# First self attention of a two-layer decoder: where in a group of four heads two pieces of projection work stand

## The chip, the cores and the metric

The kernel runs on one core of a Trainium2 chip. The metric is the device time of one execution in microseconds (us); where a kernel is timed, it is run several times and the median counts. The profile is of one execution, and its times are counted from the start of its span.

## The reference, cut to what matters

Two decoder layers with a layer norm behind each block. The change is in the first block, a self attention with 16 heads of 64 over 4 sequences of 1024 tokens of width 256:

```python
xq = jnp.einsum('bsh,oh->bso', x, wq)
xk = jnp.einsum('bsh,oh->bso', x, wk)
xv = jnp.einsum('bsh,oh->bso', x, wv)
# each reshaped to (bsz, N_HEADS, seqlen, HEAD_DIM)
scores = jax.nn.softmax(jnp.einsum('bhid,bhjd->bhij', xq, xk) * SCALE, axis=-1)
out = jnp.einsum('bhij,bhjd->bhid', scores, xv).reshape(bsz, seqlen, N_HEADS * HEAD_DIM)
x = _layernorm(x + jnp.einsum('bso,ho->bsh', out, wo))
```

The reshape doesn't transpose, so one "head" is 64 consecutive tokens with all their 1024 projected values: 1024 rows of 64. There are 64 such heads, each an attention of 1024 by 1024.

## The kernel before, in words

`layer0_self_attention` walks 16 groups of 256 tokens, and in each group 4 heads (`group`, j = 0 to 3, here called first to fourth). While a group's heads are computed, the projections of the next group (in the fourth head: of the one after it) are made in pieces between their matmuls.

**A head.** For each of 8 blocks of keys (kc): scores in two halves (`scores`, L627, "A" and "B" operands, hi and lo parts of fp32r), two matmuls of 512 columns each; between them `step`, which calls `largest` for the **next** head: a matmul (L579) into one of the two banks of `psX`, whose row maximum VectorE takes (L584). ScalarE exponentiates the scores (L639), GpSimd adds the exponentials up (`add_up`, L655, the first add behind the second exponential), and TensorE multiplies them with the values (`values`, L667) in two batches in the middle and one at the end. Then `take_out` copies the result, and `max_rows` transposes the next head's maxima (L594), VectorE takes their minimum (L599, L600) and `masked` (L609) writes them in two halves into `qB`, which the second half of the next head's scores reads. `masked` has two inputs in SBUF, `nT` and `rowmask`.

**Loads.** `build` (L538) issues from SP, right behind a head's last scores, six DMAs of 256 KB with the operands of the head after the next, into the buffers that the head has just left. The first four (`qA`, `kA`) are needed by the first `largest` of the next head (semaphore `a0` or `a1`). `build_v` (L562) loads the values of the next head in the middle of a head.

**Pieces.** `SLOTS` gives places in a group to tasks: 16 pieces Q and K (`misc`, L417: six matmuls of 256 columns, a copy `ph` on ScalarE, L458, the subtraction `pl` on VectorE, L462, and two stores of 128 KB from SP, L491), four pieces V (L425: six matmuls of 512 columns, a copy on ScalarE, L471), one T (transposes of x) and two O (output projection, L436). Places "k6", "k1" and so on stand behind that block's scores; "1", "2", "2b" in the middle; "3" to "3d" at the head's end, behind `max_rows`. A piece writes the bank `psM`, or `psX` 1 at "3b" and `psX` 0 at "3c". VectorE runs in program order; at the ends of the second and fourth head that order is: the subtraction of "3", the first mask, those of "3b" and "3c", the second mask, that of "3d".

**Waits for a bank.** VectorE's tasks on the pieces count up the semaphore `md`, ScalarE's alone (V, T) `ma`. `misc` lets TensorE wait for all of them but the last `back` ones: `under` counts how many pieces came since the one that used the same bank. `back` in `step` does the same for `largest`, whose banks are `psX` 0 and 1.

**Other work on VectorE.** In the second and fourth head `moments` (L498, L500) stands behind the second block's scores: layer norm statistics of an output tile. In the second head V stands there too ("k1").

Of the kernel before, what the change touches and what calls it, by code (L numbers as in the profile page):

```python
# [300 lines left out]
def layer0_self_attention(nc, x, wqT, wkT, wvT, woT, y):  # L301
# [13 lines left out]
    with ExitStack() as ctx:  # L315
# [44 lines left out]
        psX = m.ps("psX", [P, 2, 512])  # L360
# [8 lines left out]
        def task_list():  # L369

            slots = dict(zip(PLACES, QK, strict=True))
            slots[0, "3d"] = slots[2, "3b"] = ("O",)
            slots[2, "3"] = ("T",)
            for n, place in enumerate(((0, "k6"), (1, "k1"), (2, "k6"), (2, "k7"))):
                slots[place] = ("V", n // 2, n % 2)
            return slots

        AHEAD = 5
        QK = [("Q", c) for c in range(KC)] + [("K", c) for c in range(KC)]
        PLACES = [(3, "1"), (3, "3"), (3, "3b"), (3, "3c"), (3, "3d"), (0, "1"), (0, "2"), (0, "2b"), (0, "3"), (0, "3b"),  # L380
                  (1, "1"), (1, "3"), (1, "3b"), (1, "3c"), (1, "3d"), (2, "1")]
        SLOTS = task_list()

        def load_x(w, g):
# [182 lines left out]
        def largest(w, i, b, back=None):  # L567


            u, half = i // 2, i % 2  # L570
            if w.on("tensor"):
                if i == 0:
                    w.wait(f"fa{b}", 8 * 16)
                    w.wait(f"a{b}", w.at(f"a{b}"))
                    w.wait("mn", w.at("mn"))
                if back is not None:
                    w.wait("md", w.at("md", back))
                w.wait("mxr", w.at("mxr", 1))
                w.eng.matmul(psX[:, half, :], qA[:, b, u * P:(u + 1) * P], kA[:, b, half * 512:(half + 1) * 512],  # L579
                             start=True, stop=True).then_inc(sems["mx"], 1)  # L580
            w.inc("mx")
            if w.on("vector"):
                w.wait("mx", w.at("mx"))
                w.eng.tensor_reduce(nmax[:, half, u:u + 1], psX[:, half, :], AX.X, ALU.max, negate=True)\  # L584
                    .then_inc(sems["mxr"], 1)
            w.inc("mxr")
# [27 lines left out]
        def scores(w, kc, b, a):  # L614

            half = kc % 2
            if w.on("tensor"):
                if a == 0:
                    if kc == 0:
                        w.wait(f"fb{b}", 4 * 16)  # L620
                        w.wait(f"b{b}", w.at(f"b{b}"))
                    w.wait("e", w.at("e", 1))
                kt, qt = (kB, qB) if a else (kA, qA)
                for q in range(2):
                    if a and kc == 0:
                        w.wait("mb", w.at("mb", 1 - q))
                    last = w.eng.matmul(psS[:, half, q, :], kt[:, b, kc * P:(kc + 1) * P], qt[:, b, q * 512:(q + 1) * 512],  # L627
                                        start=a == 0, stop=a == 1)
                if a:
                    last.then_inc(sems["s"], 1)  # L630
            if a == 0:
                return
            w.inc("s")
            n = w.count.get("e", 0) % RING
            if w.on("scalar"):
                w.wait("s", w.at("s"))
                w.wait("pv", w.at("pv", {0: 3, 1: 2}.get(kc, 1 - kc % 2)))
                w.wait("ad", w.at("ad", 3 if kc in (0, 5, 6, 7) else 2))
                w.eng.activation(pr[:, n, :], psS[:, half, :, :].rearrange("p a b -> p (a b)"), ACT.Exp, scale=SCALE)\  # L639
                    .then_inc(sems["e"], 1)  # L640
            w.inc("e")
# [59 lines left out]
        def group(w, G, first=False, left=2):  # L701
            last = left == 0

            for j in range(GH):
                more = not (last and j == GH - 1)
                b, nb = j % 2, (j + 1) % 2
                old = not (first and j == 0)
                def step(i):
                    if not more:
                        return  # L710
                    before = (j - 1) % GH
                    back = None
                    if (i == 0 and (before, "3c") in SLOTS) or (i == 1 and (before, "3c") not in SLOTS):
                        back = int((before, "3d") in SLOTS and not (first and j == 1))
                    if i == 13 and (j, "2b") in SLOTS:
                        back = 0
                    largest(w, i, nb, back)

                def piece(where, bank=None, under=(0, 0)):


                    task = SLOTS.get((j, where))
                    ahead = 2 if task == ("T",) or j == 3 else 1
                    if task is None or (not old if task[0] == "O" else ahead > left):
                        return under
                    if task[0] == "O":
                        misc(w, task, G - (j == 0), 1 if j == 0 else 0, bank=bank, back=under)
                    else:
                        misc(w, task, G + ahead, (G + ahead) % 2, bank=bank, back=under)
                    return under[0] + int(task[0] in "QKO"), under[1] + {"T": 2, "V": 1}.get(task[0], 0)  # L730

                for p in range(KC // 2):
                    for kc in (2 * p, 2 * p + 1):
                        scores(w, kc, b, 0)
                        step(2 * kc)
                        scores(w, kc, b, 1)
                        add_up(w, kc, j % 2)
                        outs = j % 2 == 1 and not (first and j == 1)
                        if outs and kc == 2:
                            root(w, 1 if j == 1 else 0)  # L740
                        if outs and kc == 5:
                            norm_out(w, G - (j == 1), 1 if j == 1 else 0)
                        if kc == KC - 1 and not (last and j >= 2):
                            build(w, G + (j + 2) // GH, (j + 2) % GH, b)
                        step(2 * kc + 1)
                        if outs and kc == 1:
                            moments(w, 1 if j == 1 else 0)
                        piece(f"k{kc}")
                        if old and kc == 4:
                            turn_back(w)  # L750
                        if old and kc == 5:
                            divide(w, (j - 1) % GH)
                    if p == 1:
                        piece("1")
                    if p in (1, 2):
                        values(w, 2 * p - 2, b)
                        values(w, 2 * p - 1, b)
                        if p == 1 and old:
                            misc(w, ("S",), G, (j + 1) % 2)
                        if p == 1 and more:  # L760
                            build_v(w, (j + 1) % GH, nb)
                    if p == 2:
                        under = piece("2")
                        if w.on("tensor") and (j, "2b") in SLOTS:
                            w.wait("mxr", w.at("mxr"))
                        piece("2b", bank=psX[:, 1, :], under=under)
                for kc in range(KC - 4, KC):
                    values(w, kc, b)
                take_out(w)
                if more:  # L770
                    max_rows(w, nb)
                rest_first = left > 0 and SLOTS.get((j, "3"), ("T",))[0] in "QK"
                if more and not rest_first:
                    masked(w, nb, 0)
                    masked(w, nb, 1)
                first_d, first_a = under = piece("3")
                if more and rest_first:
                    masked(w, nb, 0)
                under = piece("3b", bank=psX[:, 1, :], under=under)
                if w.on("tensor") and (j, "3c") in SLOTS:  # L780
                    w.wait("mn", w.at("mn"))
                under = piece("3c", bank=psX[:, 0, :], under=under)
                if more and rest_first:
                    masked(w, nb, 1)
                piece("3d", under=(under[0] - first_d, under[1] - first_a))
                if j == 1 and not last:
                    load_x(w, G + 2)

# [2060 lines left out]
```

## Time and profile before

| | |
|---|---|
| median of 3 runs | 3000.15 us (2994.0 to 3001.02) |
| profiled execution | 2996.25 us, its span 2994.5 us |
| first self attention | from the start to about 1730 us |
| TensorE busy, share of the span | 88% |
| VectorE, ScalarE, GpSimd busy | 57%, 39%, 53% |
| granted clock, mean | 0.942 of full speed |

Rows of a timeline give the start in us, the duration in us, the engine, the line of the kernel, the operation, and what it writes and reads; xN joins N instructions of a kind that follow each other. Matmuls overlap in the array, so their durations are longer than the distance from one start to the next. In brackets stands the idle time of the engine before the row, and what ended it. PE is TensorE, DVE VectorE, ACT ScalarE, POOL GpSimd, SP the queue that issues DMAs; `a_` is the prefix of this stage's tiles.

### The profile page before, as it was taken

How to read it: one execution, taken by the hardware profiler on the slowest of the kernel's cores; microseconds unless marked ns; L12 is line 12 of the kernel's file. 1: busy time of each engine (PE TensorE's matmuls, PEld its weight loads, DVE VectorE, ACT ScalarE, POOL GpSimd, SP SyncE). 2: the span in 40 equal slices, each digit the busy share in tenths (PEclk: the TensorE clock that was granted, in tenths of full speed). 3: DMA queues.
4: the chain of work that ended last, by engine and by line, in shares of the span. 5: the costliest groups of instructions: out<-in, count | busy, mean ns of one | idle time of the engine just before them, and what ended most of it. 6: DMA issues, size and time to landing. Idle time of an engine off the chain costs nothing. (4 is left out here: it accounts for less than half of the span.)

```text
span 2994.5 us, 43256 instructions
## 1 busy us (share of the span) xinstructions
PE 2639.8 (88%) x11953; PEld 1603.3 (54%) x11953; DVE 1699.4 (57%) x3404; ACT 1175.7 (39%) x1644; POOL 1574.1 (53%) x1309
## 2 busy tenths in 40 slices
PE   7999999999999999999999968882796588788696
PEld 5666666666666666666666533432474244343254
DVE  5665665656666665665666634663234555468743
ACT  3443444444444444444444324541222334344234
POOL 3666766767766677676777731224333313222343
PEclk8999999999999999999999979996898599899798
DMA  6554455554556445455554320003894100000233
GB/s 174 115 130 111 105 121 114 120 116 110 113 114 135 108 111 120 106 121 114 122 115 106 68 82 9 2 2 116 334 339 144 45 0 1 30 2 9 49 124 91
DMA packets 407008, 303.17 MB, mean 101 GB/s; under 512 B 293559, under 2 KB 338911, under 8 KB 401791
## 3 DMA queue, kind: packets, MB, share of 16 engines
q1 hardware_dynamic: 390734, 231.17, 32.9%
q0 software_dynamic: 12224, 64.71, 6.1%
q10 hardware_dynamic: 3952, 6.08, 0.6%
q8 instruction: 50, 0.82, 0.1%
q14 instruction: 48, 0.39, 0.1%
HBM read 187.04 MB, written 94.39 MB: 94 GB/s over the span
## 5 line engine op out<-in xcount | busy, mean ns | idle before, releaser
L655 POOL TENSOR_TENSOR a_total<-a_total,a_pr 128x1024 f32<-128x1024 f32 x384 | 914.0, 2380 | 55.9 <-ACT a_pr L639 35.1
L639 ACT ACTIVATE a_pr<-a_psS 128x1024 f32<-128x1024 f32 x512 | 525.3, 1027 | 670.3 <-PE a_psS L627 666.5
L584 DVE TENSOR_REDUCE a_nmax<-a_psX 128x1 f32<-128x512 f32 x1024 | 695.4, 688 | 157.4 <-PE a_psX L579 155.8
L667 PE MATMUL a_psO<-a_pr,a_vd 128*64 128x512 f32 x2048 | 481.8, 602 | 0.0
L579 PE MATMUL a_psX<-a_kA,a_qA 128*128 128x512 f32 x1024 | 413.1, 405 | 25.6 <-issue 12.6
L655 POOL TENSOR_TENSOR a_total<-a_pr 128x1024 f32<-128x1024 f32 x64 | 153.5, 2399 | 482.0 <-ACT a_pr L639 482.0
L627 PE MATMUL a_psS<-a_qA,a_kA 128*128 128x512 f32 x1024 | 338.9, 412 | 2.7 <-DVE a_nT L600 1.4
L627 PE MATMUL a_psS<-a_qB,a_kB 128*128 128x512 f32 x1024 | 321.2, 395 | 0.0
L667 PEld LDWEIGHTS a_psO<-a_pr,a_vd 128*64 128x64 f32 x2048 | 129.9, 136 | 236.5 <-issue 179.3
L579 PEld LDWEIGHTS a_psX<-a_kA,a_qA 128*128 128x128 f32 x1024 | 194.0, 190 | 105.8 <-issue 35.9
L627 PEld LDWEIGHTS a_psS<-a_qA,a_kA 128*128 128x128 f32 x1024 | 180.9, 189 | 123.1 <-issue 90.1
L627 PEld LDWEIGHTS a_psS<-a_qB,a_kB 128*128 128x128 f32 x1024 | 193.2, 189 | 39.4 <-DVE a_qB L609 1.2
L1076 POOL CAST c_qR<-c_qF 128x512 fp32r<-128x512 f32 x64 | 39.4, 615 | 207.5 <-ACT c_qF L1071 207.5
L1092 DVE TENSOR_REDUCE c_nmx<-c_psM 128x4 f32<-128x308 f32 x256 | 110.1, 467 | 63.3 <-PE c_psM L1087 61.8
L599 DVE COPY a_nT<-a_psX 8x128 f32<-8x128 f32 x64 | 17.8, 279 | 222.3 <-PE a_psX L594 222.3
L1066 PE MATMUL c_psM<-c_xT,c_wq 128*128 128x512 f32 x256 | 120.3, 607 | 5.4 <-ACT c_xT L1053 5.4
L475 DVE STREAM_TRANSPOSE a_turned<-a_psM 128x512 f32<-128x512 f32 x64 | 45.9, 717 | 135.8 <-PE a_psM L430 135.8
L1087 PE MATMUL c_psM<-c_kblk,c_qR 128*128 128x308 f32 x256 | 92.7, 401 | 27.9 <-DVE c_nmx L1092 14.3
L677 ACT ACTIVATE a_oU<-a_psO 128x512 f32<-128x512 f32 x64 | 38.3, 599 | 184.1 <-PE a_psO L667 180.1
L462 DVE TENSOR_TENSOR a_pl<-a_psM,a_ph 128x256 fp32r<-128x256 f32 x150 | 63.1, 421 | 81.2 <-ACT a_ph L458 81.2
L1087 PEld LDWEIGHTS c_psM<-c_kblk,c_qR 128*128 128x128 f32 x256 | 46.1, 191 | 112.9 <-issue 91.3
L1215 POOL TENSOR_TENSOR c_rstd<-c_mv,c_eps 128x2 f32<-128x2 f32 x32 | 6.3, 196 | 186.6 <-DVE c_mv L1206 186.5
(390 smaller groups left out, 4344.7 us busy)
## 6 DMA issues: line engine op xcount, KB each, us to landing
a_qA<-a_qhi SPq DMA_DIRECT2D x124, 256.0 KB
a_vd<-a_vg SPq DMA_DIRECT2D x128, 128.0 KB
a_kA<-a_khi SPq DMA_DIRECT2D x62, 256.0 KB
a_kA<-a_klo SPq DMA_DIRECT2D x62, 256.0 KB
a_kB<-a_khi SPq DMA_DIRECT2D x62, 256.0 KB
a_qB<-a_qlo SPq DMA_DIRECT2D x62, 256.0 KB
a_qhi<-a_ph SPq DMA_DIRECT2D x120, 128.0 KB, 3.1
a_qlo<-a_pl SPq DMA_DIRECT2D x120, 128.0 KB, 2.9
```

The costliest lines, as they stand in the source:

```text
L462: w.eng.tensor_tensor(pl[:, n, :], ps[:, 0:GT], ph[:, n, :].bitcast(F32), ALU.subtract)\
L475: w.eng.transpose(turned[:, :], ps[:, :]).then_inc(sems["md"], 1)
L579: w.eng.matmul(psX[:, half, :], qA[:, b, u * P:(u + 1) * P], kA[:, b, half * 512:(half + 1) * 512], start=True, stop=True).then_inc(sems[" ...
L584: w.eng.tensor_reduce(nmax[:, half, u:u + 1], psX[:, half, :], AX.X, ALU.max, negate=True)\
L627: last = w.eng.matmul(psS[:, half, q, :], kt[:, b, kc * P:(kc + 1) * P], qt[:, b, q * 512:(q + 1) * 512], start=a == 0, stop=a == 1)
L639: w.eng.activation(pr[:, n, :], psS[:, half, :, :].rearrange("p a b -> p (a b)"), ACT.Exp, scale=SCALE)\
L655: w.eng.tensor_tensor(total[:, buf, :], first, pr[:, n, :], ALU.add).then_inc(sems["ad"], 1)
L667: last = w.eng.matmul(psO[q * HD:(q + 1) * HD, :], vd[:, b, kc, :], pr[:, n, q * 512:(q + 1) * 512], start=kc == 0, stop=kc == KC - 1)
L1066: last = w.eng.matmul(psM[:, k, :], wq[:, cc, c * P:(c + 1) * P], xT[:, cc, :], start=cc == 0, stop=cc == 1)
L1076: w.eng.tensor_copy(qR[:, n % 2, c, :], qF[:, n % 3, c, :]).then_inc(sems["qr"], 1)
L1087: w.eng.matmul(psM[:, k, 0:K4], qR[:, n % 2, c, tt * P:(tt + 1) * P], kblk[:, c, b, :, :].rearrange("p i k -> p (i k)"), start=True, stop= ...
L1092: w.eng.tensor_reduce(nmx[:, tt, 4 * c:4 * c + 4], psM[:, k, 0:K4].rearrange("p (i k) -> p i k", k=TK), AX.X, ALU.max, negate=True).then_i ...
```

## The change

Two things move. In the fourth head (j = 3) the piece Q at "1", in the middle, goes, and the five Q pieces stand at "3", "3b", "3c", "3d" and a new place "3e". In the second head (j = 1) the piece V at "k1" goes to "3d", and the K piece that was there to "3e". "3e" writes `psX` 1, the bank of "3b", and its `under` lets the two pieces since "3b" be open in the fourth head, one of each kind in the second: the subtraction of "3b" must be done. The first `largest` of the next head (`psX` 0) now lets the pieces behind "3c" be open, and the second (`psX` 1) waits for all of them.

```diff
-            for n, place in enumerate(((0, "k6"), (1, "k1"), (2, "k6"), (2, "k7"))):
+            for n, place in enumerate(((0, "k6"), (1, "3d"), (2, "k6"), (2, "k7"))):
...
-        PLACES = [(3, "1"), (3, "3"), (3, "3b"), (3, "3c"), (3, "3d"), (0, "1"), (0, "2"), (0, "2b"), (0, "3"), (0, "3b"),
-                  (1, "1"), (1, "3"), (1, "3b"), (1, "3c"), (1, "3d"), (2, "1")]
+        PLACES = [(3, "3"), (3, "3b"), (3, "3c"), (3, "3d"), (3, "3e"), (0, "1"), (0, "2"), (0, "2b"), (0, "3"), (0, "3b"),
+                  (1, "1"), (1, "3"), (1, "3b"), (1, "3c"), (1, "3e"), (2, "1")]
...
-                        back = int((before, "3d") in SLOTS and not (first and j == 1))
+                        later = [SLOTS[before, where][0] for where in ("3d", "3e") if (before, where) in SLOTS]
+                        back = sum(t in "QKO" for t in later) if not (first and j == 1) else 0
+                    elif i == 1 and (before, "3e") in SLOTS:
+                        back = 0
...
-                first_d, first_a = under = piece("3")
+                past_3 = piece("3")
...
-                under = piece("3b", bank=psX[:, 1, :], under=under)
+                past_3b = piece("3b", bank=psX[:, 1, :], under=past_3)
...
-                under = piece("3c", bank=psX[:, 0, :], under=under)
+                past_3c = piece("3c", bank=psX[:, 0, :], under=past_3b)
...
-                piece("3d", under=(under[0] - first_d, under[1] - first_a))
+                after_3 = piece("3d", under=tuple(a - b for a, b in zip(past_3c, past_3)))
+                piece("3e", bank=psX[:, 1, :], under=tuple(a + b - c for a, b, c in zip(after_3, past_3, past_3b)))
```

## Rows read from the trace of the kernel before

**Rows 1.** The page's first part: busy us, share of the span, instructions.
```profile
PE 2639.8 (88%) x11953; PEld 1603.3 (54%) x11953; DVE 1699.4 (57%) x3404; ACT 1175.7 (39%) x1644; POOL 1574.1 (53%) x1309
```
**Rows 2.** Windows, two of them a head to its `max_rows`: busy us, clock, DMA, GB/s.
```profile
233.00:1600.00 1367.00, 1352.62 (x6434) 867.85 (x6432) 843.51 (x1503) 583.99 (x773) 946.56 (x516) 1.00 0.51 116
989.66:1010.68 21.02, 20.94 (x92) 11.91 (x90) 13.62 (x24) 9.00 (x10) 16.43 (x11) 1.00 0.22 54
1043.15:1065.12 21.97, 21.97 (x98) 13.11 (x96) 13.74 (x24) 9.57 (x11) 16.74 (x12) 1.00 0.34 79
```
**Rows 3.** Waits of TensorE from 233 to 1600: us in total, times, longest.
```profile
PE a_psX L579 <- issue: 4.6, 12, 0.5
PE a_psX L579 <- DMA a_kA<-a_klo: 4.3, 8, 0.8
...
PE a_psX L579 <- DVE a_pl L462: 1.6, 5, 0.4
```
**Rows 4.** Timeline of TensorE, end of a fourth head and start of the next.
```profile
1013.06 0.40 PE L417 MATMUL a_psM<-a_xh,a_wqh 128*128 128x256 f32 x2
...
1013.78 0.63 PE L627 MATMUL a_psS<-a_qA,a_kA 128*128 128x512 f32 x2
1014.79 0.49 PE L579 MATMUL a_psX<-a_kA,a_qA 128*128 128x512 f32 x1 [0.38 <-DMA a_kA<-a_klo]
...
1016.27 0.40 PE L579 MATMUL a_psX<-a_kA,a_qA 128*128 128x512 f32 x1
```
**Rows 5.** Timeline of TensorE, second head and start of the third.
```profile
1046.10 0.63 PE L425 MATMUL a_psM<-a_wvh,a_xh 128*128 128x512 f32 x2
...
1047.48 0.61 PE L627 MATMUL a_psS<-a_qA,a_kA 128*128 128x512 f32 x2
...
1068.21 0.63 PE L627 MATMUL a_psS<-a_qA,a_kA 128*128 128x512 f32 x2
1069.38 0.49 PE L579 MATMUL a_psX<-a_kA,a_qA 128*128 128x512 f32 x1 [0.54 <-issue]
...
1070.87 0.40 PE L579 MATMUL a_psX<-a_kA,a_qA 128*128 128x512 f32 x1
```
**Rows 6.** Timelines of VectorE and GpSimd at the ends of the same two heads.
```profile
1012.57 1.21 DVE L609 TENSOR_TENSOR a_qB<-a_nT,a_rowmask 8x512 fp32r<-8x512 f32 x1
1013.72 0.74 DVE L462 TENSOR_TENSOR a_pl<-a_psX,a_ph 128x256 fp32r<-128x256 f32 x2
1014.38 0.67 DVE L609 TENSOR_TENSOR a_qB<-a_nT,a_rowmask 8x512 fp32r<-8x512 f32 x1
1014.98 0.40 DVE L462 TENSOR_TENSOR a_pl<-a_psM,a_ph 128x256 fp32r<-128x256 f32 x1
...
1008.41 4.83 POOL L655 TENSOR_TENSOR a_total<-a_total,a_pr 128x1024 f32<-128x1024 f32 x2
...
1062.51 4.82 POOL L655 TENSOR_TENSOR a_total<-a_total,a_pr 128x1024 f32<-128x1024 f32 x2
```
**Rows 7.** Timelines of GpSimd and VectorE in the last group, which has no pieces.
```profile
1645.36 4.85 POOL L655 TENSOR_TENSOR a_total<-a_total,a_pr 128x1024 f32<-128x1024 f32 x2
...
1647.88 3.47 DVE L609 TENSOR_TENSOR a_qB<-a_nT,a_rowmask 8x512 fp32r<-8x512 f32 x2
```
**Rows 8.** Timelines at a first head's end: two pieces and O.
```profile
1038.68 0.40 PE L417 MATMUL a_psX<-a_xh,a_wkh 128*128 128x256 f32 x2
...
1039.30 0.42 DVE L462 TENSOR_TENSOR a_pl<-a_psM,a_ph 128x256 fp32r<-128x256 f32 x1 [0.54 <-ACT a_ph L458]
...
1039.78 3.72 PE L436 MATMUL a_psM<-a_wo,a_oT 128*128 128x256 f32 x16 [0.22 <-DVE a_pl L462]
```
**Rows 9.** Timeline of TensorE: first L579 of the third head, groups 0 and 1.
```profile
83.03 0.47 PE L579 MATMUL a_psX<-a_kA,a_qA 128*128 128x512 f32 x1 [1.30 <-issue]
...
216.18 0.49 PE L579 MATMUL a_psX<-a_kA,a_qA 128*128 128x512 f32 x1 [2.10 <-issue]
```

## The prediction, made before the changed kernel was run

> **What bounds the kernel now.** The page first: TensorE is busy 88% of the span [rows 1]. The change touches the first stage alone, so I asked for busy time by stretch: from 233 to 1600 us TensorE works 1352.62 of 1367 us at a granted clock of 1.00 [rows 2]. This stage is a packed stream of matmuls, and the change removes none. It can only win or lose idle time between them.
>
> So the waits of TensorE come next: in those 1367 us they are short and almost all stand before L579, the row-maximum matmul of `largest`: 4.6 + 4.3 + 1.6 = 10.5 us in 25 waits, 0.42 each, released by "issue", by the DMA of `kA` or by a subtraction on DVE [rows 3]. The timeline shows where: at the start of the first and of the third head of a group, behind an end with four Q/K pieces. In the group that I use throughout, the fourth head's `max_rows` starts at 1010.68 [rows 2], the next head's first score matmul at 1013.78, its first L579 at 1014.79 and its third at 1016.27 [rows 4]. A matmul of 512 columns starts every 0.23 us (V's six take 1.38, [rows 5]), and the third L579 is the ninth matmul from the first score, so without a wait it would come 8 x 0.23 = 1.85 later, at 1015.63. The second head's end shows the same: 1068.21, 1069.38, 1070.87, so 2.66 instead of 1.85 [rows 5]. I measure everything by this third L579, because the restart after a wait is then paid (1.48 from the first L579 to the third, where six matmuls take 1.38: 0.1).
>
> What does the wait stand for? `build` issues the loads of `kA` and `qA` right behind a head's last scores, and the next head's first L579 needs them. With more matmuls between the last scores and that L579, the loads land in time. That is what the change gives: one Q/K piece (0.72 us, [rows 4]) goes behind the scores of the fourth head, and one V piece (1047.48 - 1046.10 = 1.38, [rows 5]) behind those of the second.
>
> **The second engine in this picture** is GpSimd. `masked` on VectorE (L609) takes 0.67 alone, but 1.21 at 1012.57, ending at 1013.78; GpSimd's last add pair ends at 1008.41 + 4.83 = 1013.24 [rows 6]. So the mask ends 0.54 after the add. In the last group a pair of masks started at 1647.88 and took 3.47: it hardly moved until the adds ended at 1650.21, and then took 1.14 [rows 7]. I read a hold until the add ends, not a slowing. If it were a slowing, by the 0.13 us of work that got done in 0.67 of overlap [rows 6], the mask discussed below would end 0.14 earlier, and my sum would be 2 us lower. The Trainium skill, SBUF — State Buffer, section "Who interferes with whom", says the same as the first reading: a VectorE instruction with two SBUF inputs and a GpSimd one that reads SBUF take the shared ports as an exclusive lock for the whole instruction. By that rule a mask that is ready sooner gains nothing, which speaks against this change. By it, the trace agrees: 2.3 us of hold in [rows 7].
>
> **End of the fourth head (14 times).** Removed: piece "1" in the middle, 0.72 of TensorE. Added: piece "3e" at the end, same 0.72. TensorE's work up to the next head's start is thus unchanged, and `max_rows` comes 0.72 earlier, at 1009.96. GpSimd's chain of adds does not get earlier: it starts with the second exponential, early in the head, and runs on without a gap to 1013.24. So mask one still ends at 1013.78, though it is ready 0.72 sooner. Behind it on VectorE stand the subtractions of "3b" and "3c": the pair takes 0.74 from 1013.72, a single one 0.40, so that of "3b" ends at 1014.12 [rows 6]. Now the new piece "3e" writes the bank `psX` 1 that "3b" used, and its `under` makes TensorE wait until the subtraction of "3b" is done. TensorE could start it at 1013.06 (four pieces after 1010.68 - 0.72, [rows 4]). After a subtraction TensorE resumes 0.06 later (1039.30 + 0.42 against 1039.78, [rows 8]), so "3e" starts at 1014.18: **a new wait of 1.1 us**, in front of everything else. Then 0.72 + 0.1 for piece and restart: scores at 1015.00, first L579 at 1015.46 (the loads, issued 0.72 earlier, are in), second at 1016.15, third at 1016.85. The other new wait, of the second L579 for all subtractions, is just met: a piece's subtraction ends 1.04 after its matmuls (1038.68 to 1039.72, [rows 8]), at 1016.04. Against 1016.27 before: +0.58, 14 times, +8.1 us.
>
> **The second head (15 times).** V leaves the place behind the second scores. What it covered there is VectorE's `moments`; uncovered, the head is the same sequence as the fourth one now, which takes 21.02 from first scores to `max_rows` where this takes 21.97 [rows 2]. So only 0.95 of the 1.38 is saved, and 0.43 is lost in the middle. `max_rows` at 1065.12 - 0.95 = 1064.17; the old four pieces' span of 3.09 and V's 1.38 bring the scores to 1068.64. GpSimd: in the fourth head its chain ends 1013.24 - 989.66 = 23.58 after the head's start; from 1043.15 that gives 1066.73, against 1062.51 + 4.82 = 1067.33 now [rows 2, 6]. Mask one ends at 1067.27, "3b"'s subtraction at 1067.61, and "3e" would start at 1068.64 - 0.72 = 1067.92: no wait, by 0.25 (less the 0.06). The loads, issued 0.95 earlier, landed at the latest at 1069.38 before, now at 1068.43: in time. The last subtraction, 1068.64 + 1.04 = 1069.68, is ready for the second L579 at 1069.80. Third L579 at 1070.49 against 1070.87: -0.38. In groups 0 and 1 the load was later (waits of 1.30 and 2.10, [rows 9]) and I count -1.4 and -1.2 there; in the fifteenth the wait was about nothing, +0.2. Sum: 12 x -0.38 - 2.6 + 0.2 = -7.0 us.
>
> The DMAs: each moved Q/K piece sends two 128 KB stores from SP's queue. At the fourth head's end five pairs now follow the loads, none ahead of them, and what is queued behind them on SP is a piece in the middle of the next head. I cost this at nothing; if the stores did hold up the loads, see the third rival. ScalarE's copies move with their pieces; it is busy 583.99 of 1367 us [rows 2]. V moves past `build_v` of the third head, which reads other rows, so nothing waits for it.
>
> One correction: my group's waits (0.38 and 0.54, mean 0.46) are longer than the mean of 0.42, so the kernel before is 0.04 faster at 26 starts, +1.0 us. **Sum: 8.1 - 7.0 + 1.0 = +2.1 us.** The profiled execution took 2996.25 (span 2994.5), the median of the three runs is 3000.15, 3.9 above it; I put the difference on the median: 3002.3.
>
> Bounds: the new wait of "3e" is 1.1 by the hold; with no hold it would be 0 (first rival), and I take the hold, for its row is the same instruction at the same place. Each 0.1 in either chain is 1.4 us.
>
> **Rivals.**
> *Faster: no wait at "3e".* If the subtraction of "3b" were not held (a mask that gets its turn before the last add, or an `under` that allows more), scores stay at 1013.78 and the third L579 comes at 1015.63: -0.64, 14 times, -9.0 us; with the second head's -7.0 and the correction, -15.0: **2985**. For it: the waits of 25 starts are all that the change aims at. Against: 0.54 behind the add in both rows, and the add before ends near 1010.83, a microsecond before mask one can be ready. Chance 0.10.
> *Slower: the new wait in the second head too.* The place is "3e" behind V. It has 0.2 us to spare. If GpSimd's chain does not get earlier when V leaves (end at 1067.33), mask one ends at 1067.87, "3b" at 1068.21, "3e" starts at 1068.27 instead of 1067.92: 0.35 and 0.1 restart, 15 times, +6.8; in sum +8.9: **3009.1**. It decides from 0.2 us of delay on. For it: gaps of GpSimd between adds are set by exponentials, which I moved by inference only. Against: the fourth head has this sequence already and no gap. Chance 0.13.
> *Loads land no earlier*, because the engines that carry them share with other traffic. The first L579 of the third head stays at 1069.38, its gain of 0.38 and the extra in two groups are gone: 8.1 + 1.0 = +9.1, **3009.2**. For it: landings scatter. Against: nothing new is ahead of them. Chance 0.07.
> My forecast has 0.70.
>
> **The numbers.** What a measurement of this kernel tells from no change is 0.3%, 9 us. My forecast's own spread is some 4 us, so it lies inside almost wholly; the slower rivals stand at that bound and go over it in some two of three cases (0.13), with 0.04 from the forecast's tail: slower 0.17. Faster 0.11, same 0.72. Range 2993 to 3011: it takes in the slower rivals and leaves out the faster one.
>
> **What would show it.** TensorE's waits list a new row on L417 into `psX`, released by a subtraction (L462), 14 times and 1.0 to 1.1 each; the waits before L579 are nearly gone; the second head lasts 21.0 from first scores to `max_rows`, the fourth 20.3; the mask at the fourth head's end takes about 1.9. A mask of 0.67 there, or no wait before "3e", would prove me wrong to the fast side; a wait of "3e" behind V to the slow side.

## The result, and the profile after

| | before | changed |
|---|---|---|
| median, 22 runs each | 2994.81 us | 3000.68 us |
| ratio | | 1.0018, interval 1.0010 to 1.0026 |
| span of the profiled execution | 2994.5 us | 2999.2 us |

The changed kernel is slower by 0.18%, some 5 us (the two medians differ by 5.9): inside the 0.3% that the forecast called no change, on the slower side as its sum of +2.1 us said, and somewhat more than that sum. The 22 runs of the kernel before have a median 5 us below that of the three shown ahead of the prediction, so the forecast's absolute time (3002.3) is to be read as its distance.

TensorE's waits from 233 to 1600 us of the changed kernel (us in total, times, longest), the same view as [rows 3]:

```profile
PE a_psX L417 <- DVE a_pl L462: 12.9, 13, 1.0
PE a_psM L436 <- DVE a_pl L462: 2.8, 13, 0.2
```

All three rows of waits before L579 (10.5 us, 25 times) are gone. In their place stands one that [rows 3] had not: a piece's matmul into `psX` that waits for a subtraction, 13 times in this stretch, 12.9 us. The timeline of TensorE at a fourth head's end shows which:

```profile
1010.42 0.38 PE L594 MATMUL a_psX<-a_ident,a_nmax 128*8 128x128 f32 x2
...
1013.27 0.40 PE L417 MATMUL a_psM<-a_xh,a_wql 128*128 128x256 f32 x2
1014.65 0.51 PE L417 MATMUL a_psX<-a_xh,a_wqh 128*128 128x256 f32 x2 [0.98 <-DVE a_pl L462]
...
1015.47 0.62 PE L627 MATMUL a_psS<-a_qA,a_kA 128*128 128x512 f32 x2
1015.93 0.40 PE L579 MATMUL a_psX<-a_kA,a_qA 128*128 128x512 f32 x1
...
1016.64 0.49 PE L579 MATMUL a_psX<-a_kA,a_qA 128*128 128x512 f32 x1
1016.97 0.62 PE L627 MATMUL a_psS<-a_qA,a_kA 128*128 128x512 f32 x2
1017.42 0.39 PE L579 MATMUL a_psX<-a_kA,a_qA 128*128 128x512 f32 x1
```

Four pieces follow `max_rows` without a gap, then the fifth, "3e", starts 1.38 after the last pair before it instead of 0.24, so the wait moves it by 1.14. The first L579 comes 0.46 after the scores, where [rows 4] had 1.01. VectorE and GpSimd at the same end:

```profile
1011.97 0.42 DVE L462 TENSOR_TENSOR a_pl<-a_psM,a_ph 128x256 fp32r<-128x256 f32 x1 [0.54 <-ACT a_ph L458]
1012.31 1.95 DVE L609 TENSOR_TENSOR a_qB<-a_nT,a_rowmask 8x512 fp32r<-8x512 f32 x1
1014.19 0.74 DVE L462 TENSOR_TENSOR a_pl<-a_psX,a_ph 128x256 fp32r<-128x256 f32 x2
...
1016.08 0.42 DVE L462 TENSOR_TENSOR a_pl<-a_psX,a_ph 128x256 fp32r<-128x256 f32 x1 [0.23 <-ACT a_ph L458]
...
1008.86 4.85 POOL L655 TENSOR_TENSOR a_total<-a_total,a_pr 128x1024 f32<-128x1024 f32 x2
```

The mask takes 1.95 where [rows 6] had 1.21: it was ready 0.74 sooner and ends where it ended before, 0.55 behind GpSimd's add (1013.71 to 1014.26). The subtraction of "3b", first of the pair behind it, ends at about 1014.59, and "3e" starts 0.06 later.

At the second head's end there is no wait. GpSimd's last pair of adds there, in its timeline, ends at 1063.07 + 4.82 = 1067.89:

```profile
1063.07 4.82 POOL L655 TENSOR_TENSOR a_total<-a_total,a_pr 128x1024 f32<-128x1024 f32 x2
```

The windows (busy us of the engines, clock, DMA share, GB/s), which answer to [rows 2], give both heads' lengths:

```profile
990.12:1010.42 20.30, 20.21 (x87) 11.05 (x85) 13.17 (x23) 8.69 (x9) 15.72 (x11) 1.00 0.16 44
1044.32:1065.35 21.03, 20.94 (x92) 11.92 (x90) 13.60 (x24) 8.98 (x10) 16.47 (x11) 1.00 0.35 83
```

The fourth head is shorter by its piece (20.30 against 21.02), the second by 0.94 of V's 1.38, as the forecast had from the fourth head's row.

### The profile page after: what moved, and what is told of

Its sections match the earlier page's. It is cut to its first block and busy times, and to the rows that moved or that the text cites. A ratio compares the mean times of both kernels' runs of the same rounds, so it can differ in the third digit from the quotient of the medians.

```text
span 2999.2 us, 43301 instructions
## 1 busy us (share of the span) xinstructions
PE 2641.8 (88%) x11953; PEld 1600.7 (53%) x11953; DVE 1712.2 (57%) x3404; ACT 1177.0 (39%) x1644; POOL 1574.7 (53%) x1309
## 5 line engine op out<-in xcount | busy, mean ns | idle before, releaser
L579 PE MATMUL a_psX<-a_kA,a_qA 128*128 128x512 f32 x1024 | 413.5, 405 | 13.6 <-issue 5.7
L579 PEld LDWEIGHTS a_psX<-a_kA,a_qA 128*128 128x128 f32 x1024 | 193.8, 189 | 94.2 <-DVE a_nmax L584 24.5
L609 DVE TENSOR_TENSOR a_qB<-a_nT,a_rowmask 8x512 fp32r<-8x512 f32 x128 | 118.2, 934 | 0.7
```

What stands on the lines that cost most here:

```text
L609: w.eng.tensor_tensor(qB[0:KC, b, cols].rearrange("p (u q) -> p u q", q=P), nT[:, 1, :].unsqueeze(1).to_broadcast([KC, KC // 2, P]), rowma ...
```

## How the kernels are compared below

A ratio covers the whole kernel, so beside each stands the length of a group in the profiled execution. It is the distance from the fourth head's `max_rows` in group 1 to that in group 13 (groups counted from 0, as in [rows 9]), divided by 12. In the kernel before: (1542.22 - 265.48) / 12 = 106.40 us; in the changed one (1544.55 - 262.49) / 12 = 106.84. The heads' parts are means over these groups: first the length of the head, from its first scores to `max_rows`, then the "end", from `max_rows` to the next head's third L579.

| kernel | ratio, interval | group | 2nd head, end | 4th head, end |
|---|---|---|---|---|
| before | 1 | 106.40 | 21.98, 5.58 | 21.03, 5.66 |
| changed | 1.0018, 1.0010 to 1.0026 | 106.84 | 21.01, 6.38 | 20.29, 7.02 |
| v_only | 0.9980, 0.9970 to 0.9991 | 106.24 | 21.02, 6.37 | 21.04, 5.64 |
| q_only | 1.0024, 1.0012 to 1.0035 | 107.13 | 22.01, 5.69 | 20.34, 6.94 |
| mask_late | 0.9976, 0.9965 to 0.9986 | 106.17 | 21.01, 6.37 | 20.33, 6.30 |
| mask_psum | 0.9954, 0.9939 to 0.9970 | 105.71 | 21.02, 6.37 | 20.32, 5.84 |
| before_mask_psum | 1.0003, 0.9992 to 1.0013 | 106.32 | 21.98, 5.56 | 21.03, 5.61 |
| no_last_add | 0.9947, 0.9931 to 0.9964 | 105.62 | 21.01, 6.37 | 20.29, 5.81 |
| moments_late | 1.0015, 1.0006 to 1.0024 | 106.79 | 20.64, 6.60 | 19.94, 7.46 |
| both | 0.9924, 0.9908 to 0.9939 | 104.96 | 20.64, 6.37 | 19.96, 5.86 |

## Experiments 1 and 2: each half alone

v_only takes from the change only the V move (and "3e" in the second head):

```diff
-        PLACES = [(3, "3"), (3, "3b"), (3, "3c"), (3, "3d"), (3, "3e"), (0, "1"), (0, "2"), (0, "2b"), (0, "3"), (0, "3b"),
+        PLACES = [(3, "1"), (3, "3"), (3, "3b"), (3, "3c"), (3, "3d"), (0, "1"), (0, "2"), (0, "2b"), (0, "3"), (0, "3b"),
```

> The V half of the change alone: V behind the second head's end, K piece at "3e"; the fourth head as before. My theory (the two halves add up; the second head loses 0.43 in the middle and gains back the load wait): second head 21.0 us from first scores to max_rows, 4.5 from there to the next scores, no wait before "3e", third L579 some 0.15 us earlier per group than before, and 2 us once in group 1 where the load was late: 2 to 5 us faster than before (ratio 0.9985 to 0.9995). Rival (the uncovered moments are what makes the changed kernel slower): 15 x 0.43 = 6 us slower than before, ratio 1.002. The loads' rival (they land no earlier): no difference.

q_only takes only the Q move:

```diff
-            for n, place in enumerate(((0, "k6"), (1, "3d"), (2, "k6"), (2, "k7"))):
+            for n, place in enumerate(((0, "k6"), (1, "k1"), (2, "k6"), (2, "k7"))):
...
-                  (1, "1"), (1, "3"), (1, "3b"), (1, "3c"), (1, "3e"), (2, "1")]
+                  (1, "1"), (1, "3"), (1, "3b"), (1, "3c"), (1, "3d"), (2, "1")]
```

> The Q half alone: the fourth head's middle piece at its end, as "3e"; V stays at "k1". My theory: the wait of 1.0 us before "3e" stands 14 times; from max_rows to the third L579 of the next head 7.0 us against 5.65 before, 0.71 of it won back in the middle: +0.6 to +0.7 per group, 8 to 10 us slower than before (ratio 1.0027 to 1.0033). Rival (the V half carries the loss): this half is at or under the kernel before, since its load waits of 0.6 are gone: ratio 0.998 to 1.000.

v_only is faster than the kernel before (0.9980), q_only slower (1.0024), so the change is a gain and a larger loss. The rivals that gave the loss to V, or called both nothing, are out. The group tells the same: -0.16 and +0.73, whose sum of +0.57 is near the +0.44 of the whole; the rest I leave open (the load waits differ from execution to execution). q_only's waits of TensorE from 233 to 1600 show the new wait beside those which the second head's untouched end still has:

```profile
PE a_psX L417 <- DVE a_pl L462: 11.9, 13, 1.0
PE a_psX L579 <- issue: 4.3, 10, 0.6
```

Both missed their ranges a little on the fast side: v_only 0.9980 where 0.9985 was the edge, q_only 1.0024 where 1.0027 was. In the profiled executions a part of v_only's gain is a stretch of low clock in group 1 of the kernel before, 1.2 us, which is shown further down.

## Experiment 3: the mask behind the subtraction of "3b"

Is it the order on VectorE that makes "3e" wait?

```diff
-                if more and rest_first:
-                    masked(w, nb, 0)
                 past_3b = piece("3b", bank=psX[:, 1, :], under=past_3)
+                if more and rest_first:
+                    masked(w, nb, 0)
```

> The changed kernel with one order changed on VectorE: the first mask behind the subtraction of "3b" instead of ahead of it. My theory ("3e" waits only for that subtraction, which stands behind the held mask): the wait before "3e" is gone, scores come at max_rows + 3.9 in place of + 5.05. But the mask still ends 0.54 behind GpSimd's last add and with it the second mask and the subtractions behind it, so part comes back as a wait of 0.3 to 0.6 before the first or second L579: 5 to 10 us faster than the changed kernel, 0 to 5 faster than before (ratio 0.998 to 1.000). Rival A (the wait before "3e" is ScalarE's or the bank's, not the order behind the mask): unchanged, ratio 1.002. Rival B (all of the 1.1 us comes back behind the later waits, since the held mask sets everything): ratio 1.001 to 1.002.

0.9976: by the ratios 12.6 us under the changed kernel and 7 under the one before, each a little beyond the range expected; by the groups, 14 x 0.67 = 9.4 us under the changed one. The first theory holds, and some of the 1.1 us comes back as later waits. The timelines of VectorE and TensorE at a fourth head's end:

```profile
1007.09 1.18 DVE L609 TENSOR_TENSOR a_qB<-a_nT,a_rowmask 8x512 fp32r<-8x512 f32 x1
1008.20 0.41 DVE L462 TENSOR_TENSOR a_pl<-a_psX,a_ph 128x256 fp32r<-128x256 f32 x1
1008.53 0.67 DVE L609 TENSOR_TENSOR a_qB<-a_nT,a_rowmask 8x512 fp32r<-8x512 f32 x1
...
1009.47 0.40 DVE L462 TENSOR_TENSOR a_pl<-a_psX,a_ph 128x256 fp32r<-128x256 f32 x1
```
```profile
1008.29 0.63 PE L627 MATMUL a_psS<-a_qA,a_kA 128*128 128x512 f32 x2
...
1010.00 0.50 PE L579 MATMUL a_psX<-a_kA,a_qA 128*128 128x512 f32 x1 [0.23 <-DVE a_pl L462]
```

The five pieces now run through (scores 3.81 after `max_rows` at 1004.48). But the mask is still held, and the second L579 waits for the last subtraction, which ends at 1009.87 behind both masks. This is the second new wait of the change; in the changed kernel the first one covers it, all but the 0.1 of a restart (below).

## Experiments 4 to 6: is it a hold by GpSimd's add?

mask_psum writes the minimum into `psO`, which is free between `take_out` and the next `values`, so that the mask has one operand in SBUF and one in PSUM:

```diff
+                w.wait("nm", w.at("nm"))
-                w.eng.tensor_tensor(nT[:, 1, :], nT[:, 0, :], psX[0:KC, 0, P:2 * P], ALU.min)
+                w.eng.tensor_tensor(psO[0:KC, 0:P], nT[:, 0, :], psX[0:KC, 0, P:2 * P], ALU.min)
...
-                                    nT[:, 1, :].unsqueeze(1).to_broadcast([KC, KC // 2, P]),
+                                    psO[0:KC, 0:P].unsqueeze(1).to_broadcast([KC, KC // 2, P]),
...
+                    w.wait("mb", w.at("mb"))
```

The last line lets the next `values` wait until the masks have read that bank.

> The changed kernel with the minimum of the maxima written to psO, a PSUM bank that is free there, so that the mask reads one operand from PSUM and one from SBUF. My theory (GpSimd's add holds a VectorE instruction with two SBUF inputs until it ends): the mask takes 0.67 to 0.75 everywhere, also under a running add; no wait before "3e"; scores at max_rows + 3.8 to 3.9, all three L579 without a wait. Against the changed kernel -1.3 us in 14 groups and up to 3 us more at the last groups' ends, where masks of 2.7 to 3.5 were held: 18 to 24 us faster than it, 13 to 19 faster than before (ratio 0.994 to 0.9955). Rival (the mask is long because GpSimd's traffic slows any VectorE access, PSUM or not): the mask keeps its 1.9 us and the time is that of the changed kernel, 1.002.

0.9954, at the slow edge of the range expected. No mask is long any more. The rows of the mask's line from 233 to 1600 (min, median and max ns), first of mask_late, then of mask_psum:

```profile
L609 DVE TENSOR_TENSOR a_qB<-a_nT,a_rowmask x104: 668/673/1200, 238.2 to 1593.0; 8x512 fp32r<-8x512 f32 x104
```
```profile
L610 DVE TENSOR_TENSOR a_qB<-a_psO,a_rowmask x104: 668/669/679, 238.8 to 1587.1; 8x512 fp32r<-8x512 f32 x104
```

And an add runs over the mask as before. GpSimd and VectorE at one end of mask_psum:

```profile
1000.05 4.84 POOL L656 TENSOR_TENSOR a_total<-a_total,a_pr 128x1024 f32<-128x1024 f32 x2
```
```profile
1003.55 0.67 DVE L610 TENSOR_TENSOR a_qB<-a_psO,a_rowmask 8x512 fp32r<-8x512 f32 x1
```

The add ends at 1004.89, the mask has run from 1003.55 to 1004.22 under it. In the last group, where [rows 7] had 3.47 for a pair of masks, it takes 1.28 now:

```profile
1636.43 1.28 DVE L610 TENSOR_TENSOR a_qB<-a_psO,a_rowmask 8x512 fp32r<-8x512 f32 x2
```

The same edit in the kernel before asks whether the hold cost anything there:

> The kernel before with the mask's operand in PSUM. My theory (before the change the loads set the next head's start, not the held mask): the mask takes 0.7 everywhere, yet from max_rows to the third L579 behind the fourth head it stays 5.6 to 5.66 us, released by the DMA of kA; only the last group's ends get shorter, 3 us in all as in the changed kernel with the same edit. Ratio 0.998 to 0.9992. Rival (the held mask costs the kernel before as much as the changed one): another 0.5 us or more per group, ratio 0.9955 to 0.9965.

1.0003, interval 0.9992 to 1.0013: no difference. This was half a miss: the held mask is worth nothing in the groups, but I had expected the last group's shorter masks to show as 0.08% to 0.2% and they don't in this ratio. In the profiled executions the stretch from the third L579 behind group 14's second head to the last head's first scores is 119.74 us where the kernel before has 121.51, so 1.8 us shorter; the interval leaves room for 2.4, so the ratio can't tell this gain from none. The rival (0.9955 to 0.9965) is excluded. All masks are at 0.67 to 0.68 there too, and the waits before L579 stay what they were in [rows 3]:

```profile
PE a_psX L579 <- issue: 4.7, 14, 0.5
PE a_psX L579 <- DMA a_kA<-a_klo: 3.4, 8, 0.5
...
PE a_psX L579 <- DVE a_pl L462: 1.4, 2, 0.7
```

So before the change the held mask stood in the shadow of the late load; the change took the shadow away.

no_last_add comes from the other side: the mask keeps both operands in SBUF, and the changed kernel's GpSimd doesn't add the last block's exponentials (the sum lacks one block of eight):

```diff
+            if kc == KC - 1:
+                if w.on("gpsimd"):
+                    w.wait("e", w.at("e"))
+                    w.wait("ad", w.at("ad"))
+                    w.eng.tensor_tensor(mhalf[:, :], mhalf[:, :], zero[:, :], ALU.add).then_inc(sems["ad"], 1)
-            if w.on("gpsimd"):
+            elif w.on("gpsimd"):
```

> The changed kernel without GpSimd's last add of each head (the eighth block's exponentials are left out of the sum; a tiny add stands for its semaphore). The mask keeps its two SBUF inputs. My theory (the hold lasts as long as the add runs): GpSimd's chain ends 2.4 us earlier, the mask at the fourth head's end takes 0.67, the wait before "3e" is gone, max_rows to scores is 3.8 us as with the operand in PSUM: 16 to 30 us faster than the changed kernel (the last group, where TensorE waits for the sums, gains too), ratio 0.990 to 0.996. Rival (the mask is long for a reason of its own, its operands' layout or its place behind max_rows): mask 1.9 and wait 1.0 stay, ratio at 1.000 or above.

0.9947, the end behind the fourth head 5.81, as with the operand in PSUM (5.84), and the same mask on the same data now never exceeds 0.68:

```profile
L609 DVE TENSOR_TENSOR a_qB<-a_nT,a_rowmask x104: 669/671/678, 239.5 to 1587.0; 8x512 fp32r<-8x512 f32 x104
```

Two edits that share nothing but the hold remove the same wait. The Trainium skill's SBUF — State Buffer, section "Who interferes with whom", has both sides of it: a VectorE instruction with two SBUF inputs contends with a GpSimd instruction that reads SBUF; one with at most one SBUF input, outside the 2-port perf modes, does not. The runs agree: 1.95 against 0.67 under an add.

## Experiments 7 and 8: the uncovered moments, and the best version

moments_late puts `moments` and `root` behind the fourth block's scores, where `values` follows and VectorE has time:

```diff
-                        if outs and kc == 2:
-                            root(w, 1 if j == 1 else 0)
...
-                        if outs and kc == 1:
+                        if outs and kc == 3:
                             moments(w, 1 if j == 1 else 0)
+                            root(w, 1 if j == 1 else 0)
```

> The changed kernel with moments (and root) behind the fourth block's scores instead of the second's. My theory (uncovered moments delay the row maxima behind them, and TensorE waits for a bank of psX): the 0.35 to 0.43 us in the middle of the second and fourth head are gone (20.6 and 19.9 us to max_rows). At the fourth head's end nothing is won, since GpSimd's chain is fixed there: the wait before "3e" grows to 1.35. At the second head's end "3e" has 0.25 to spare before it waits for the same reason, so 0.2 to 0.3 of 0.43 stays. In all 2 to 5 us faster than the changed kernel, ratio 1.0000 to 1.0012. Rival (moments cost nothing; the 0.43 is V's own exponential order): head lengths unchanged, ratio 1.0018.

1.0015, above the range expected (1.0000 to 1.0012) and its interval reaching over that of the changed kernel: most of the expected gain did not come. The heads did get shorter, by 0.37 and 0.35, so the moments' part of the theory holds, and its rival is out. At the fourth head's end all of the 0.35 came back (end 7.46 for 7.02), as the mask was ready sooner still and held as long as before. Another 0.1 came on top: counted from the head's first scores, the held mask there ends at 24.21 in the mean of twelve groups, where it is 24.14 in the changed kernel. At the second head's end 0.23 came back, since "3e" waits there too now. This kernel's mask and waits from 233 to 1600, and the second head's "3e" in the timeline:

```profile
L609 DVE TENSOR_TENSOR a_qB<-a_nT,a_rowmask x103: 668/673/2606, 238.2 to 1599.2; 8x512 fp32r<-8x512 f32 x103
```
```profile
PE a_psX L417 <- DVE a_pl L462: 18.5, 13, 1.6
```
```profile
1066.89 0.62 PE L425 MATMUL a_psM<-a_wvh,a_xl 128*128 128x512 f32 x2
1067.48 0.51 PE L417 MATMUL a_psX<-a_xh,a_wkh 128*128 128x256 f32 x2
```

The pair of V's matmuls takes 0.46, so 0.13 is wait, and the next pair starts 0.35 later instead of 0.24.

both joins this with the mask's operand in PSUM:

> The changed kernel with the mask's operand in PSUM and moments behind the fourth block. My theory (the two are independent once no mask is held): third L579 as early as in the PSUM kernel, and 0.35 to 0.43 less in 29 heads' middles: 10 to 12 us faster than the PSUM kernel, ratio 0.991 to 0.993. Rival (the loads, issued earlier still relative to nothing else, set the start again): the gain comes back as waits before the first L579, ratio 0.995.

0.9924: the fastest, some 22 us under the kernel before and, by the ratios, 9 under mask_psum (by the groups 14 x 0.75 = 10.5). What was lost in moments_late is won here: heads of 20.64 and 19.96 and ends of 6.37 and 5.86. Hardly a wait is left from 233 to 1600:

```profile
PE a_psM L436 <- DVE a_pl L462: 2.8, 13, 0.2
PE a_psX L579 <- DVE a_pl L462: 0.4, 1, 0.4
```

## Why the prediction was right

Its steps, with what they measured:

- **"3e" waits behind the fourth head, 14 times.** Forecast: "3e" starts 1.12 late, and 0.1 of restart follows; measured 1.14 (of which the trace shows 0.98 as idle time) and 0.1. Scores at `max_rows` + 5.04; measured 5.05. Shown by its row, by mask_late (order), mask_psum and no_last_add (hold).
- **GpSimd's chain keeps its time.** End at 23.58 after the second head's start: measured 1067.89 - 1044.32 = 23.57. In the fourth head the held mask ends 24.14 after the first scores in both kernels (means of twelve groups). "3e" behind V has a little to spare: no wait there, and moments_late, 0.37 shorter, has one. So the slower rival's mechanism exists and its point lies close, but the change stays short of it.
- **V's place covered the moments.** 0.95 of 1.38 saved: 21.03 for the second head. moments_late wins all but 0.04 of the rest (20.64).
- **Loads land in time.** No wait before L579 from 233 to 1600; the rival of loads that land no earlier falls. Group 0 is an exception, see below.
- **The faster rival** needed a mask that is not held. Its ends would be 1.85 after scores; mask_psum gives 2.03, so it was 0.18 too cheap, but of the right kind: 0.9954 measured (with 3 us of it from the last group's masks), 0.995 forecast.

**What was mis-sized.** The sum said +2.1, the profiled spans differ by 4.7 (2999.2 - 2994.5), the ratio says 5.4. In the two traces the distance from one head's third L579 to the next one's changes as follows, up to the second head's end of group 14 (us, changed kernel minus the one before, rounded; the correction of +1.0 is split by its 14 and 12 starts):

| heads | forecast | measured |
|---|---|---|
| fourth, 14 of them | 8.1 + 0.6 | 8.8 |
| second, groups 2 to 13 | -4.6 + 0.5 | -2.1 |
| second, group 0 | -1.4 | -0.1 |
| second, group 1 | -1.2 | -2.2 |
| second, group 14 | +0.2 | +0.2 |
| third | 0 | -1.1 |
| first, and the start | 0 | +0.4 |
| sum | +2.1 | +4.0 |

The other 0.7 between the spans lies behind this point.

1. **Group 0.** The wait of 1.30 at 83.03 [rows 9] stands at the end of the **first** head, not of the second; [rows 9] and the forecast put it at the wrong one. Nothing was won there: the wait is 1.63 in the changed kernel, which is most of the +0.4.

```profile
83.51 0.47 PE L579 MATMUL a_psX<-a_kA,a_qA 128*128 128x512 f32 x1 [1.63 <-issue]
```

2. **Second heads of groups 2 to 13.** The example's load wait was the longer kind: from scores to third L579 2.66 us, where the mean before is 2.49. The correction of 0.04, taken from all waits together, gave back too little of these 0.17.
3. **Fourth heads.** Their sum fits, but two errors cancel in it. The example's load wait was 0.08 shorter than the mean here (2.49 against 2.57). And the second new wait, of the second L579 for all subtractions, was forecast as just met, at no cost. It is just met: the last subtraction ends at 1016.50, and that L579 starts at 1016.64 with no idle time shown. Yet the matmul after it starts 0.33 later (at 1016.97) where 0.23 is the rule, as after a wait. The end is 7.02 where the steps gave 1016.85 - 1009.96 = 6.89. The weight loads of the first and second L579 show a difference:

```profile
1015.73 0.19 PEld L579 LDWEIGHTS a_psX<-a_kA,a_qA 128*128 128x128 f32 x1
...
1016.63 0.19 PEld L579 LDWEIGHTS a_psX<-a_kA,a_qA 128*128 128x128 f32 x1 [0.28 <-issue]
```

The first starts 0.20 ahead of its matmul, the second 0.01: the load waited too. That this is where the 0.1 comes from is a reading; no run isolates it.

4. **Group 1.** The forecast's -1.2 does not follow from its own rows: with a wait of 2.10 in place of 0.54 the gain is 0.38 + 1.56, so -1.9 (and group 0 would have been -1.1). Measured are -2.2, and the third head's -1.1 belongs here as well. Behind its wait of 2.10 the kernel before ran at the lower of TensorE's two clock levels (0.50, 1.2 GHz) for some 3 us, which the forecast, with rows from 233 on, did not look at. Windows of the kernel before, then of the changed one:

```profile
213.00:216.00 3.00, 1.07 (x8) 0.64 (x6) 1.71 (x5) 0.69 (x2) 0.00 (x0) 1.00 1.10 210
216.00:218.00 2.00, 1.82 (x7) 1.46 (x8) 1.29 (x2) 0.75 (x1) 0.00 (x0) 0.83 0.93 211
218.00:220.00 2.00, 2.00 (x6) 1.59 (x5) 0.90 (x3) 0.74 (x2) 0.00 (x0) 0.50 0.97 219
```
```profile
218.00:220.00 2.00, 2.00 (x11) 1.63 (x10) 2.00 (x4) 1.66 (x2) 0.96 (x1) 1.00 0.90 198
```

From that third L579 to the next `max_rows` it took 22.58 us before (217.93 to 240.51) and 21.31 after (216.96 to 238.27), 1.27 less. In the other eight profiled executions, where the clock is 1.00 there, it is shorter by 1.2 to 1.3 too. Whether the clock falls in other executions of the kernel before isn't known.

So the mechanism held in each main step, while that the sum came as near as it did is in part luck: its errors pull both ways. The verdict of "no change" had room for them, as each is about 2 us or less and the bound was 9.

## What to carry to other kernels

A late load can hide a second limit just behind it. Before adding cover for the load, follow what each bank of the added work waits for, and through which queue: here the fifth piece reused the bank of the second, whose release stood behind an instruction held by another engine. Where a held VectorE instruction is on such a path, look whether one of its inputs can stand in PSUM: this edit alone turned the change from 0.2% slower to 0.5% faster, and was worth nothing in the kernel before, where the load still ruled.

## What the runs showed of the hardware

- A VectorE `tensor_tensor` with two SBUF inputs that is ready while a GpSimd add runs ends 0.53 to 0.56 us behind that add, however long the wait: 1.21, 1.95 and, in moments_late, up to 2.6 us for an instruction of 0.67 (a pair of masks ends 1.14 to 1.15 behind it). With one input in PSUM it takes 0.67 to 0.68 under the add. The hold appears in the trace as the instruction's own duration, not as idle time before it.
- Behind a wait of TensorE for a semaphore the next step took about 0.1 us longer: 0.34 instead of 0.24 behind "3e" (1014.65 to 1014.99), 0.33 instead of 0.23 behind the second L579, where no idle time is shown.
- Behind a wait of 2.10 us (TensorE busy 1.07 of 3.00 us from 213 to 216) the granted clock of the kernel before fell from 1.00 to 0.50, the level of the whole stretch from 218 to 220 us; from 221 us on it was 1.00 again. Behind the third L579 alone this cost 1.3 us. In no_last_add the same followed a wait of 1.79 us in group 0 (0.50 from 86 to 88 us).
